# The dt projection of a Mamba and mixture-of-experts kernel over 64 rows in place of 16

## The reference

```python
xz = x @ in_proj_w.T                       # 256 -> 2 * 512
xc, z = jnp.split(xz, 2, axis=-1)
xc = _silu(conv(xc) + conv_b)              # depthwise, 4 taps, causal
dbc = xc @ x_proj_w.T                      # 512 -> 16 + 16 + 16
dt, Bm, Cm = jnp.split(dbc, [DT_RANK, DT_RANK + D_STATE], axis=-1)
dt = jax.nn.softplus(dt @ dt_proj_w.T + dt_proj_b)     # 16 -> 512
...
dA = jnp.exp(dt_t[..., None] * A)
h = dA * h + (dt_t * x_t)[..., None] * B_t[:, None, :]
y = jnp.einsum('bdn,bn->bd', h, C_t)
```

## Time and profile before

| | |
|---|---|
| median of three runs | 5189.0 us (5183.5 to 5210.0) |
| profiled execution, own time | 5185.9 us |
| its span, first to last instruction | 5184.2 us |
| TensorE busy, share of the span | 82% |
| VectorE busy | 84% |
| ScalarE busy | 68% |
| GpSimd busy | 69% |
| mean granted clock of TensorE | 0.915 |

### The profile page before, as it was taken

One profiled execution on the slowest core, in us unless ns is written; L12 is line 12 of the kernel. 1 busy time (PEld: TensorE's weight loads), 2 busy tenths in 40 slices (PEclk: granted clock), 3 DMA queues, 4 the chain that ended last, 5 costly groups with the idle time before them and its releaser, 6 DMA issues. The chain is left out here.

```text
span 5184.2 us, 75345 instructions
## 1 busy us (share of the span) xinstructions
PE 4226.3 (82%) x20862; PEld 2939.7 (57%) x20862; DVE 4336.0 (84%) x6189; ACT 3531.4 (68%) x6409; POOL 3559.4 (69%) x2235
## 2 busy tenths in 40 slices
PE   4778788788888888888888888888888888888874
PEld 2455555565555556555565555565565666656652
DVE  4899998988888898888888888888898888888742
ACT  4666666676666667767677667677767777776742
POOL 4666666666666667766777767677777786687853
PEclk6889998999899999898899999899999999999998
DMA  2122322343333323332333333333334443555662
GB/s 93 60 69 88 109 86 82 109 128 120 103 123 112 123 68 113 99 102 82 103 88 90 109 102 91 94 100 87 100 111 126 128 126 104 140 147 146 171 170 60
DMA packets 348416, 551.94 MB, mean 106 GB/s; under 512 B 39377, under 2 KB 196178, under 8 KB 347874
## 3 DMA queue, kind: packets, MB, share of 16 engines
q1 hardware_dynamic: 279026, 448.92, 28.2%
q0 software_dynamic: 47616, 65.17, 6.3%
q10 hardware_dynamic: 21360, 33.03, 1.7%
HBM read 432.78 MB, written 181.33 MB: 118 GB/s over the span
## 5 line engine op out<-in xcount | busy, mean ns | idle before, releaser
L568 POOL TENSOR_TENSOR dBx<-dtx,Bbc 128x1024 f32<-128x1024 f32 x1024 | 2430.5, 2422 | 714.9 <-DVE hs L1180 699.6
L1180 DVE TENSOR_TENSOR_SCAN hs<-ps,dBx 128x512 f32<-128x512 f32 x2048 | 2400.8, 1207 | 221.9 <-ACT ps L722 107.0
L722 ACT ACTIVATE ps<-dt,A 128x512 f32<-128x512 f32 x2048 | 1392.5, 689 | 595.1 <-DVE hs L1180 567.2
L935 PE MATMUL ps<-ident,hs 128*128 128x128 f32 x8192 | 1341.5, 303 | 495.7 <-DVE acc L1196 388.2
L935 PEld LDWEIGHTS ps<-ident,hs 128*128 128x128 f32 x8192 | 1037.0, 154 | 970.6 <-DVE acc L1196 617.8
L1196 DVE SCALAR_TENSOR_TENSOR acc<-ps,C_tok,acc 128x512 f32<-128x512 f32 x1792 | 1276.4, 738 | 263.2 <-PE ps L935 244.4
L624 POOL DMA_INDIRECT fx<-Y_slots,slots x248 | 393.8, 1588 | 105.8 <-issue 54.9
L603 POOL DMA_INDIRECT X_slots<-xs,slots x248 | 246.7, 995 | 263.2 <-DVE slots L1318 198.4
L1093 PE MATMUL ps<-xsT,wx 128*128 128x128 f32 x2432 | 324.6, 286 | 26.6 <-ACT xsT L814 26.6
L1169 DVE SCALAR_TENSOR_TENSOR xc<-ps,conv_w,xc 128x511 f32<-128x511 f32 (+2 forms) x384 | 285.9, 745 | 56.0 <-ACT xc L686 44.9
L1093 PEld LDWEIGHTS ps<-xsT,wx 128*128 128x128 f32 x2432 | 305.7, 201 | 44.6 <-issue 43.0
(11 more groups left out here) (206 smaller groups left out, 5967.8 us busy)
## 6 DMA issues: line engine op xcount, KB each, us to landing
Bbc<-B_scratch SPq DMA_DIRECT2D x512, 256.0 KB, 3.5
wx<-in_experts SPq DMA_DIRECT2D x304, 384.0 KB, 3.8
Y_slots<-zeros SPq DMA_DIRECT2D x228, 256.0 KB, 4.4
xin<-X_slots SPq DMA_DIRECT2D x304, 128.5 KB
Y_slots<-xin SPq DMA_DIRECT2D x304, 128.0 KB, 1.7
xt<-in_x SPq DMA_DIRECT2D x32, 512.0 KB, 4.0
shared<-xt ACTq DMA_DIRECT2D x31, 512.0 KB, 2.6
fx<-shared SPq DMA_DIRECT2D x31, 512.0 KB, 3.6
```

Of the source, the lines that this page charges most:

```text
L568: pool.tensor_tensor(dBx[u % 3][:], dtx[b % 2][:, 2 * h:2 * h + 2, :], Bbc[g % NBB][:, n % CH:n % CH + 1, :].broadcast_to([P, 2, T]), ALU. ...
L722: act.activation(psA[s % 2][:], dt[b % 2][:, j, :], ACT.Exp, scale=A[:, j, n:n + 1]).then_inc(s_dA, 1)
L935: i = pe.transpose(psH[w % 2][:, j * P:(j + 1) * P], hs[(n * CT + j) % NHB][:, t * P:(t + 1) * P], ident[:])
L1180: dve.tensor_tensor_scan(hs[s % NHB][:], psA[s % 2][:], dBx[s // 2 % 3][:, s % 2, :], 0.0, ALU.mult, ALU.add).then_inc(s_scan, 1)
```

## The change

The dt projection's matmul names rows 0 to 63 of `few` on both sides (`w_dt0`, `dbc0`) in place of 0 to 15. So that the added rows add nothing, VectorE first clears rows 0 to 63 of the whole tile; the dt weights are loaded into rows 0 to 15 behind that, for which SyncE waits on a new semaphore, `s_few`. Rows 16 to 63 of the weights stay zero. In the moving operand rows 16 to 47 hold B and C, and rows 48 to 63 stay zero. The output has the same 128 partitions and 512 columns. The order of the instructions on every engine is the same but for the memset at the head of VectorE's program.

```diff
--- before.py
+++ after.py
@@ -236,7 +236,9 @@
 
         few = sb("few", [P, DI + T])
         M0, B2 = 64, 96
+        M_DT = 64
         w_dt, dbc = few[0:R, 0:DI], few[0:NX, DI:DI + T]
+        w_dt0, dbc0 = few[0:M_DT, 0:DI], few[0:M_DT, DI:DI + T]
         b2 = few[B2:B2 + 1, 0:D]
         taken, table = 0, []
         for n in (NE * (CAP // P), NT, NE, NE, NE, NT * NE, NT, NT):
@@ -291,6 +293,7 @@
         s_B_in = [sem(f"B_in{i}") for i in range(NBB)]
 
         s_zeroed, s_consts, s_halved, s_A_exp = sem("zeroed"), sem("consts"), sem("halved"), sem("A_exp")
+        s_few = sem("few")
 
         s_bn_post, s_mean_post = sem("bn_post"), sem("mean_post")
         s_tap, s_scan, s_weighed = sem("tap"), sem("scan"), sem("weighed")
@@ -372,6 +375,8 @@
         @block.sync
         def _(sp):
             for dst, key_ in loads:
+                if key_ == "dt_proj_w":
+                    sp.wait_ge(s_few, 1)
                 sp.dma_start(dst if key_ == "dt_proj_w" else dst[:], a[key_]).then_inc(s_weights, 16)
             sp.dma_start(b2, a["mlp_b2"]).then_inc(s_weights, 16)
             sp.dma_start(w_shared[:], a["experts"][NE]).then_inc(s_weights, 16)
@@ -921,7 +926,7 @@
                             pe.wait_ge(s_C_tok, b + 1)
                         elif b:
                             pe.wait_ge(s_dt_relu, per_batch(b, j - 1, CT))
-                        pe.matmul(bank(b, j)[:], w_dt[:, j * P:(j + 1) * P], dbc[0:R, :], start=True, stop=True).then_inc(
+                        pe.matmul(bank(b, j)[:], w_dt0[:, j * P:(j + 1) * P], dbc0, start=True, stop=True).then_inc(
                             s_dt_mm, 1)
 
             def turn():
@@ -1141,6 +1146,7 @@
 
         @block.vector
         def _(dve):
+            dve.memset(few[0:M_DT, :], 0.0).then_inc(s_few, 1)
             dve.memset(where[0], 0).then_inc(s_consts, 1)
             dve.memset(where[1], 0).then_inc(s_consts, 1)
             for k in range(CAP // P):
```

## The result

The changed kernel takes 5147.1 us, the median of four runs (5143.6 to 5158.3), against 5186.4 us (four runs, 5183.5 to 5210.0). The ratio is 0.9919 with a 95% interval of 0.9891 to 0.9948: faster by 0.8%. The prediction was 5141, with a range of 5085 to 5195.

The account below looks back on a forecast made before the run. VectorE (84% busy) and TensorE (82%) were taken to bound the kernel by waiting on each other, TensorE slowed by low clock. Matmul and memset 0, clock 48 us off 5185.9 gave 5138, or 5141 against the median; range 5085 to 5195.

Parts of the forecast that it names:

- 0.45 us per low microsecond: Dt projection stretches, long against short: 3.05 us more time for 6.8 us more at the low clock level.
- Batch 0 as evidence: Batch 0, nothing overlapping: a busy TensorE gained the clock on the x projection's 128 rows, lost it on the dt projection's 16.
- The sign named for batch 0: If right, batch 0's low clock level begins more than 1.1 us into the dt projection.
- The matmul's price, 0 us: Dt projection's 256 matmul records: 64 rows cost the same as 16, between equal 16-row and full-row prices.
- The 6 us kept on either side: First record of each dt projection pair: its extra 105 ns could vanish or double, 6 us on the path each way.
- The full-row bound: First record of each pair: full-row records lack the 105 ns extra, so it would go, 6 us less.
- The bound of 1.2 us for the memset: Added memset at VectorE's start: 1.2 us at most, hidden by later idle time, so priced 0, or 1.2 without that cover.
- The clock term, 48 us between 36 and 60: 31 dt projection stretches: clock falls remain in many batches, but later or shorter; gain 48 us, the middle of its bounds.
- my lower bound of 36: Eighteen long dt projection stretches all become like the one between, 14.99 us: 36 us gained.
- The clock never falls there: Rival, 0.16: 64 rows act as 128, so short dt projection stretches gain too, 34 on top of 60; 5095 us.
- Nothing changes: Rival, 0.24: zero rows may not be seen as work, or half the rows may be too few; 5189 us, give or take 6.
- The falls move, and the kernel is slower: Rival, 0.08: shorter batches meet new clock falls elsewhere, 3.1 us each; one in each of 31 batches gives 5236 us.

Follow-up runs that it names:

- e4: Changed kernel with the dt projection over 128 rows, tables and bias moved, bfloat16 scratch tile, memset of 128 rows: 5105.6 us, ratio 0.9846 to the kernel before.
- e9: As e4, but the dt projection over 96 rows: 5106.6 us, ratio 0.9867 to the kernel before.
- e1: Changed kernel with its memset, semaphore and wait, but the dt projection over 16 rows again: 5201.4 us, ratio 1.0038 to the kernel before.
- e3: Changed kernel with 64 rows in batches 1 to 31 and 16 in batch 0: ratio 0.9939 to the kernel before.
- e5: As e1 (16 rows), but the memset clears another buffer, so the rows below the 16 are not cleared: ratio 1.0018 to the kernel before.
- e7: As e1 with its memset, but the dt projection over 32 rows: 5202.3 us, ratio 1.0015 to the kernel before.
- e8: Control for e4: its moved tables, memset and bfloat16 scratch tile, but the dt projection over 16 rows: 5207.4 us, ratio 1.0023 to the kernel before.
- e10: As e8 (16 rows, moved tables), but the memset at the head of GpSimd's program instead of VectorE's: ratio 1.0003 to the kernel before.
- e2: Changed kernel with 64 rows in batch 0 alone and 16 in the 31 others: 5197.7 us, ratio 1.0027 to the kernel before.
- e6: Changed kernel with weights of rows 16 to 63 at 1.2e-6 in place of zero: ratio 0.9913 to the kernel before.
- e11: As e4 (128 rows), but the memset on GpSimd: ratio 0.9872 to the kernel before.
- e12: Changed kernel (64 rows) with its memset on GpSimd in place of VectorE: ratio 0.9933 to the kernel before.

## Why the prediction was right, and where it was not

**What bounds the kernel, and the price.** The mechanism held: rows added to one small matmul, no other work changed, and the time went with the low clock. 0.45 us per low microsecond turned 89 us into 40, with 42.1 measured. Over a wider range it is less: e4 has 187 us fewer than before and is 78.6 us shorter, 0.42; e9 has 239 fewer and is 90.8 shorter, 0.38.

**Batch 0 as evidence.** This step was weak. "A busy engine lost the clock on 16 rows" looked back only 1.1 us. The row ahead of it, of the same table as the earlier trace rows, has TensorE busy for 1.31 of 2.30 us, so a pause just before the fall wasn't excluded, and with it went the argument that the Trainium skill's busy rule disagrees with this trace:

```profile
48.40:50.70 2.30, 1.31 (x6) 0.32 (x4) 0.00 (x0) 0.81 (x2) 0.00 (x0) 1.00 0.00 0
```

It was also one sample, and the moment of the fall varies: of the seven profiled kernels with 16 or 32 rows in batch 0 (before, e1, e3, e5, e7, e8, e10) five took 5.87 to 6.51 us there and two kept the clock for most of it (3.85 and 3.79 us); all seven with 64 rows or more (after, e2, e4, e6, e9, e11, e12) took 3.70. Five of seven against none of seven does point the prediction's way, as one profile alone could not. The conclusion stands on the 31 later stretches, by rows and with their controls. That all of them meet the low clock in the kernel before didn't say by itself that rows cause it; e4, e8 and e3 do. The sign named for batch 0 (the low level begins more than 1.1 us in) came, and is again one sample.

**The matmul's price, 0 us.** Right, with the first record's 105 ns unchanged at 64 rows. The 6 us kept on either side weren't needed. The full-row bound, by which the extra would go in all 128 pairs, doesn't come true even at 128 rows: it goes only in the pairs right behind other full-row work, half of them.

**The memset and the order.** The bound of 1.2 us for the memset held (0.91), the load behind it wasn't delayed, and the cover was there. That the kernels with 16 rows and this memset are up to 0.4% slower than before was in no term of mine. If e1 is taken as the base for the rows alone, its group-mate e3 gains 1.0038 - 0.9939 = 1.0%, some 51 us, and the change as a whole less.

**The clock term, 48 us between 36 and 60.** The sum came out (39 us between the medians, 42 between the profiled spans), but not by its parts, and that is partly luck. Inside the stretches the gain was 25 us (461 in sum where I named 438), below my lower bound of 36. The step that failed is the lower bound, by which all the long stretches "become like the one between": they fell from eighteen to eight, not to none. 64 rows let the fall come as before in many batches, and then it lasts as long as before. The other 17 us came from outside the stretches; the prediction knew such changes only as a rival with the wrong sign. The low time that went there stood in the 10 us behind them (31 us of it), so the cut from the first L924 record to the last was too short for what the clock does there. With 64 rows the outside part was 9 to 19 us in four kernels (after, e3, e6, e12), in e9 it was 27.6, in e4 nothing. I can't say what it will be for a given kernel.

**The rivals.** "The clock never falls there" wasn't 64 rows' case but is nearly that of 128: 85 us gained in the stretches where the sum said 94, and 5105.6 us where it said 5095. "Nothing changes" fell with e6 and with the result; zeros count. The Trainium skill's rule on the same point ("TensorE: Matmul & The Clock Gate", section "What's actually happening") sets the clock by how busy TensorE has been and doesn't speak of rows. Taken alone it is incomplete: e8 and e4 differ only in rows and run the same records in the same order, and the clock is 0.911 against 0.932, with TensorE busy for less of the span at 128 rows (81% against 82%). "The falls move, and the kernel is slower" didn't happen as a net effect, but its ground was sound: the falls outside change by tens of microseconds.

## What to carry to other kernels

In this kernel a matmul record that contracts over 16 or 32 rows takes the same time as one over 128 (587 and 592 ns at the least), but TensorE's clock doesn't hold as well there. Where such matmuls stand, look at the granted clock, and if it falls, try padding the contraction with zero weights, to 96 or 128 rows if the tile has the room. The forecast for such a change is best made by cutting the trace into equal pieces of work, sorting them by length and granted clock, and taking the price of a low microsecond from the difference. Check the same cuts afterwards, and the few microseconds behind them, since a right total can hide a gain that came from elsewhere.

## What the runs showed of the hardware

- In this kernel the granted clock depends on how many rows the dt projection's matmuls use, at equal columns and equal order. Stretches of equal work: 16 or 32 rows 494 to 507 us in sum with a memset ahead (486 without), 64 rows 458 to 470, 96 rows 423, 128 rows 400 to 401. 32 rows are no better than 16.
- With 128 rows the low clock mostly leaves the stretches and stands in the 10 us behind them: there in 23 of 31, against 17 before and 8 with 64 rows.
- Zeros count: 48 rows of zero weights and 48 rows of 1.2e-6 give 0.923 both.
- The first of two float32 records over 16, 32 or 64 rows lasts 692 to 693 ns at the full clock. Over 96 or 128 rows it lasts 595 right behind full-row transposes, and 697 behind a wait.
- A memset of 64x1024 float32 zeros on VectorE took 0.91 us, and so did one of 128x1024 in e4.
- One and the same kernel ran at 5171 us and at 5203 to 5213 us on one chip, with its mean clock at 0.920 and at 0.906 to 0.908.
